# A decoder on one core: stand-in products, half slots and a halved load in the first attention, another order of moves in the later ones

## Chip, cores and metric

One Trainium2 chip, one of its cores. The metric is the time of one launch in microseconds on the device, from the median of several runs. TensorE (PE) multiplies, VectorE (DVE) and ScalarE (ACT) work elementwise, GpSimd (POOL) does little here, and SyncE (SP) issues nearly all DMAs.

## What is computed

A decoder of two layers, for a batch of 4, 512 positions and 256 features, all in float32. Each layer has a self attention, a cross attention to a context of 1024 positions and a third part. The residual stream is normalised ahead of each of the six stages. Cut to what matters here:

```python
# stage A: first attention, 16 heads of 64, rope; per batch element
scores = einsum('hid,hjd->hij', q, k) / 8
kerple = -p * log1p(a * |i - j|)
combined = concat([scores, kerple], over heads)        # 32 numbers per (i, j)
refined = gelu(combined @ w1 + b1) @ w2 + b2           # 32 -> 32 -> 16
out = softmax(causal(scores + kerple + refined)) @ v @ w_o
# stage B: cross attention, 16 heads of 16, 1024 keys, no mask
# stage C: attention with picked experts
# stage D: causal self attention, 16 heads of 16, rope, 512 keys
# stage E: cross attention, 16 heads of 16, 1024 keys, mask, biases
# stage F: 32 routed and 2 shared experts
```

## The kernel before

One hardware loop goes over the four batch elements; a pass runs the stages A to F one after the other, with a barrier of all engines between them. Every engine's instructions are written out by hand, each engine in its own order, and semaphores hold them together. SP's queue is one order too: a wait in it holds all DMAs behind it.

**Stage A** (lines 1332 to 1709). Queries, keys, scores and values come first. The scores of the four query tiles (key lengths L of 512, 384, 256 and 128) are stored to memory and loaded back as chunks, in which a row holds one head and one of 8 queries: 14 chunks, four for each of the three longer tiles and two for the last. Chunks 0 to 7 are of the two long tiles, 8 to 13 of the two short ones. A chunk lies in a slot of `a_fin`, chunk c in slot c % 4 (SP's `load`, line 1438). Its slot is free when the probabilities of the chunk in it before have been turned (line 1456: a wait on `bank_mm`). A chunk of a long tile is worked on in two units, one of a short tile in one: 22 units k. For each unit

- TensorE's `up` (lines 1502 to 1523) multiplies the scores (line 1514) and the distance terms (line 1521) by w1, when the chunk is loaded and the GELU of the unit before is done, because all units use the same four banks;
- ScalarE applies the GELU (line 1628); after the last unit of chunk c it takes the exponentials of chunk c - 1 (line 1618), which have another activation table;
- TensorE's `down` (lines 1525 to 1537) multiplies by w2 into banks 4 and 5, when VectorE has added the unit before (semaphore `mixed`);
- VectorE adds (line 1662), adds the biases and takes maxima (line 1668), and later scales by the inverse sums (line 1681).

Two chunks later TensorE turns the probabilities (line 1545, `turn`), VectorE copies them (line 1698), and when a query tile is complete TensorE weights the values (line 1555) and multiplies by w_o (line 1561). `turn_banks` writes this order out. In TensorE's main loop, step k runs up(k + 1), down(k) and then the turns and values that belong to the step; in the short tiles down(k) comes ahead of up(k + 1).

**Stages B, D, E** (`Attn16`, line 99, and the functions `a16_*`). TensorE projects keys and queries in tiles of 128 x 512; ScalarE copies each tile to `val` (lines 637 and 639), in stage D VectorE applies the rope instead. VectorE splits each tile into three bf16 parts: `parts` (lines 702 to 705) casts, subtracts, casts, subtracts, into KP and QP. SP moves the parts of every group of heads into the stacks KS and QS, six DMAs for a group (`a16_sp`, line 429), in the order of `self.moves` (line 114): t is the half of the heads, gr a group of 2, 2 or 4 heads. In `moves` of before that is, for each t, k0, k1, q0, q1, k2, q2. A wait for the split tile stands ahead of each group. The first score product of a group waits for its keys' and queries' twelve moves (line 506). OT lies over QP and KP, so ScalarE's first copy into it (line 681) waits for all 72 moves.

`keep_warm(count)` (line 399) issues products of 128 x 128 by 128 x 512 in bf16 whose result nobody reads, here called stand-ins. Before the first scores of B, D and E there are `WARM_STACK = 8` of them, behind a wait for all copies of V and all of `val`:

```python
pe.wait_ge(g("v_up"), c.nj // 2)
pe.wait_ge(g("val"), len(c.tiles))
keep_warm(WARM_STACK)
```

Of the kernel before, what the change touches and what calls it, by code (L numbers as in the profile page):

```python
# [98 lines left out]
class Attn16:  # L99


    def __init__(self, name, nk, causal, masked, rope, cross):
# [8 lines left out]
        else:  # L111
            self.tiles = [(kind, t, 0) for t in range(2) for kind in "kq"]
            self.split_order = [0, 1, 2, 3]
        self.moves = [(kind, t, gr) for t in range(2) for kind, gr in (("k", 0), ("k", 1), ("q", 0), ("q", 1), ("k", 2), ("q", 2))]
        self.step = 2 if rope else 1
# [19 lines left out]
    def bank(self, e):  # L135

        return 2 + e % 4 if self.cross else self.step * e % 6

    def pairs_at(self, t):
# [43 lines left out]
NE, NSH = 32, 2  # L183
WARM_LN, WARM_T, WARM_STACK = 22, 6, 8
NRING = 6
# [28 lines left out]
def decoder(nc, io, out, rounds=B):  # L214
    ctx = ExitStack()
    with ctx:
# [80 lines left out]
        for c in CFG:  # L297
            if c in STAGES:
                for n in ("proj", "val", "split", "v_mm", "v_up", "v_zero", "k_ones", *(f"stack_in{gr}" for gr in GROUP_AT.values()), "slot_mm", "slot_free",
                          "m_parts", "m_mm", "m_row", "st_mm", "exp", "pv", "o_up", "recip", "y_mm"):  # L300

                    sm[c, n] = sm["B", n] if c == "D" and "B" in STAGES else sem(f"{n}_{c}")
# [324 lines left out]
        def a16_act(act, c, n):  # L627
            m = M16
            g = lambda s: sm[c.name, s]
            def val(e):  # L630
                kind, t, f = c.tiles[e]
                act.wait_ge(g("proj"), e + 1)
                if e >= NVAL:
                    act.wait_ge(g("split"), e - NVAL + 1)
                o = m["val"][:, e % NVAL, :]
                if c.masked:
                    nc.scalar.activation(o, ps[:, c.bank(e), :], ACT.Identity, bias=(bqE if kind == "q" else bkE)[:, t:t + 1]).then_inc(g("val"), 1)
                else:
                    nc.scalar.activation(o, ps[:, c.bank(e), :], ACT.Copy).then_inc(g("val"), 1)
# [56 lines left out]
        def a16_dve(dve, ch, c):  # L696
            m = M16
            g = lambda s: sm[c.name, s]

            def parts(dst, src, rest, last_sem):  # L700

                ch.link(nc.vector.tensor_copy(dst(0), src))
                ch.link(nc.vector.tensor_tensor(rest, src, dst(0), ALU.subtract))
                ch.link(nc.vector.tensor_copy(dst(1), rest))
                nc.vector.tensor_tensor(dst(2), rest, dst(1), ALU.subtract).then_inc(last_sem, 1)

            for k, e in enumerate(c.split_order):
# [14 lines left out]
                dst = (lambda a: m["QP"][:, a, t, :]) if kind == "q" else (lambda a: m["KP"][:, a, t, f * BANK:(f + 1) * BANK])  # L722
                parts(dst, m["val"][:, e % NVAL, :], m["rest"][:, :], g("split"))

# [542 lines left out]
        def f_dve(dve, ch, n, st):  # L1267
# [58 lines left out]
            for i in range(NI):  # L1326
# [14 lines left out]
        BACK = 504  # L1341
        A_UP, A_DOWN, A_TURN = 0, 4, 6

        sk = [nc.dram_tensor(f"scores{i}", (AU * AH, AQ * (i + 1) * P), F32, kind="Internal").ap() for i in range(NI)]
        named("A", "rope", "qk_mm", "qk_up", "s_mm", "s_up", "v_mm", "v_up", "out0", "out1", "out2", "out3", "fin0", "fin1", "fin2", "fin3",
              "w1", "gelu", "w2", "mixed", "negm", "exp", "prob", "bank_mm", "bank_up")
# [5 lines left out]
        def a1_mem(sb2):  # L1352
# [19 lines left out]
                    M2["fin"][:, 1, 0:4 * TRI_L[3]]]  # L1372
        M1 = M2

        def chunk(n):
# [34 lines left out]
        DOWN_FIRST = [FIRST[c + 1] - 1 for c in range(NCHUNK - 1) if FIRST[c + 1] == LAST[c + 1]]  # L1410

        A_BANKS, BANKS_TO = turn_banks()
        BANK_OF = {u: k for k, u in enumerate(A_BANKS)}
# [8 lines left out]
        def a_sp(sp, b, n, st):  # L1422
# [38 lines left out]
        def a_pe(pe, _, n, st):  # L1461
# [40 lines left out]
            def up(k):  # L1502
                c, q0 = A_UNITS[k]
                i, r, _, L = chunk(c)
                R = SA_R[i]
                if k == FIRST[c]:
                    pe.wait_ge(g(f"fin{c % 4}"), 16 * (c // 4 + 1))
                if k:
                    pe.wait_ge(g("gelu"), k)
                for e in range(4):  # L1510
                    rows = slice(32 * e, 32 * e + 32)
                    for b in range(2):
                        first = (q0 + b * R) * L
                        nc.tensor.matmul(ps[64 * b:64 * b + 64, A_UP + e, 0:R * L], w1A[rows, 0, :], m["fin"][rows, c % 4, first:first + R * L],  # L1514
                                         start=True, stop=False, tile_position=(32 * e, 64 * b), skip_group_check=True)
# [23 lines left out]
            def turn(y, c, k):  # L1539
                _, _, _, L = chunk(c)  # L1540
                q0, j = A_TURNS[c][k]
                if k == 0:
                    pe.wait_ge(g("prob"), c + 1)
                for q in range(4):
                    last = nc.tensor.transpose(ps[:, A_TURN + y % 2, q * P:(q + 1) * P],
                                               m["fin"][:, c % 4, (q0 + q) * L + j * P:(q0 + q) * L + (j + 1) * P], ident[:, :])
                last.then_inc(g("bank_mm"), 1)
# [48 lines left out]
        def a_act(act, _, n, st):  # L1596
# [16 lines left out]
            def weights(c):  # L1613
                _, _, R, L = chunk(c)
                act.wait_ge(g("negm"), c + 1)
                for q in range(R):
                    row = m["fin"][:, c % 4, q * L:(q + 1) * L]
                    nc.scalar.activation(row, row, ACT.Exp, bias=m["nm"][:, c % 4, q:q + 1],  # L1618
# [14 lines left out]
        def a_dve(dve, ch, n, st):  # L1633
# [20 lines left out]
            def refined(k):  # L1654
# [4 lines left out]
                for b in range(2):  # L1659
                    first = q0 + b * R  # L1660
                    rows = m["fin"][:, slot, first * L:(first + R) * L]
                    nc.vector.tensor_tensor(rows, rows, ps[:, A_DOWN + b, 0:R * L], ALU.add).then_inc(g("mixed"), 1)  # L1662
                for b in range(2):
                    dve.wait_ge(g("mixed"), 2 * k + b + 1)
                    for q in range(q0 + b * R, q0 + b * R + R):
                        row = m["fin"][:, slot, q * L:(q + 1) * L]
                        t0 = BACK - i * P - AU * (r + q)
# [6 lines left out]
            def normal(c):  # L1674
# [4 lines left out]
                for q in range(R):  # L1679
                    row = m["fin"][:, slot, q * L:(q + 1) * L]  # L1680
                    last = nc.vector.tensor_scalar(row, row, m["den"][:, slot, q:q + 1], None, ALU.mult)
# [379 lines left out]
```

## Time and profile before

| | us |
|---|---|
| median of 3 runs | 4386.22 (4375.98 to 4389.01) |
| the profiled execution's own time | 4387.44 |
| its span | 4385.7 |
| TensorE matmul busy in it | 3846.2 (88%) |
| TensorE weight loads | 1821.0 (42%) |
| VectorE | 2457.8 (56%) |
| ScalarE | 1682.7 (38%) |
| GpSimd | 152.1 (3%) |
| mean granted TensorE clock, share of full | 0.932 |

The busy time of TensorE counts pipelined products, so it is an upper mark. "Granted clock" is the share of full speed, 2.4 GHz, that TensorE was given; it has two levels, the other is 1.2 GHz. One pass takes about 1,085 us, of which stage A takes some 260, B 177, C 117, D 118, E 204 and F 200. Times in the trace count from the span's start.

### The profile page before, as it was taken

How to read it: one execution, taken by the hardware profiler on the slowest of the kernel's cores; microseconds unless marked ns; L12 is line 12 of the kernel's file. 1: busy time of each engine (PE TensorE's matmuls, PEld its weight loads, DVE VectorE, ACT ScalarE, POOL GpSimd, SP SyncE). 2: the span in 40 equal slices, each digit the busy share in tenths (PEclk: the TensorE clock that was granted, in tenths of full speed). 3: DMA queues.
4: the chain of work that ended last, by engine and by line, in shares of the span. 5: the costliest groups of instructions: out<-in, count | busy, mean ns of one | idle time of the engine just before them, and what ended most of it. 6: DMA issues, size and time to landing. Idle time of an engine off the chain costs nothing.

```text
span 4385.7 us, 57351 instructions
## 1 busy us (share of the span) xinstructions
PE 3846.2 (88%) x21858; PEld 1821.0 (42%) x21938; DVE 2457.8 (56%) x6129; ACT 1682.7 (38%) x2508; POOL 152.1 (3%) x168
## 2 busy tenths in 40 slices
PE   5788888999878888899987898889998789888999
PEld 2352444345435244435533424443553342443355
DVE  5557565742365766573236675657324666666632
ACT  2744433431263443352127254225213726422511
POOL 1000020000000002000000000100000000200000
PEclk9998988999989899899999899889999989988999
DMA  5312002022321200202241210120324121012031
GB/s 180 107 37 55 17 21 51 16 90 72 124 71 41 51 17 26 51 11 98 69 143 53 51 35 17 42 45 1 105 62 152 49 58 24 18 42 45 1 112 59
DMA packets 134703, 254.40 MB, mean 58 GB/s; under 512 B 23269, under 2 KB 82661, under 8 KB 128997
## 3 DMA queue, kind: packets, MB, share of 16 engines
q1 hardware_dynamic: 134408, 250.50, 20.3%
q8 instruction: 182, 2.98, 0.3%
q14 instruction: 113, 0.92, 0.1%
HBM read 156.04 MB, written 44.04 MB: 46 GB/s over the span
## 4 chain that ended last, share of the span: by engine, by line
PE 67%; DVE 15%; ACT 6%; SPq 5%; DMA 3%; issue 3%; POOL 0%; DVEq 0%; POOLq 0%; ACTq 0%
PE ps L1207 11%; PE ps L578 7%; PE ps L1225 5%; PE ps L561 5%; SPq L429 5%; DVE mx L732 5%; PE ps L506 4%; PE ps L1555 3%; DVE ps L729 3%; PE ps L1473 3%; PE ps L402 2%; DMA a_fin<-scores 2%; ACT a_X L1628 2%; PE ps L1514 2%; PE ps L566 2%
## 5 line engine op out<-in xcount | busy, mean ns | idle before, releaser
L670 ACT ACTIVATE PT<-ps 128x1024 f32<-128x1024 f32 (+3 forms) x640 | 605.3, 959 | 480.8 <-PE ps L566 238.2
L506 PE MATMUL ps<-KS,QS 96*128 96x512 bf16 (+3 forms) x1280 | 473.7, 410 | 112.3 <-DVE mx L732 52.4
L732 DVE TENSOR_REDUCE mx<-ps 128x1 f32<-128x512 f32 (+3 forms) x768 | 438.1, 619 | 177.7 <-PE ps L506 87.5
L1207 PE MATMUL ps<-xnT,f_w 128*128 128x512 f32 x1088 | 488.8, 592 | 0.0
L561 PE MATMUL ps<-QS,KS 99*128 99x512 bf16 (+2 forms) x1280 | 431.9, 382 | 10.4 <-ACT QS L660 6.2
L729 DVE CUSTOM_DVE_ANT_0 ps<-ps,mneg 128x512 f32<-128x512 f32 x512 | 342.1, 715 | 136.8 <-PE ps L506 135.1
L578 PE MATMUL ps<-PT,VP 128*32 128x512 f32 (+3 forms) x2560 | 390.9, 593 | 18.4 <-ACT OT L681 18.1
L1313 DVE TENSOR_TENSOR f_tm<-f_si,ps 128x512 f32<-128x512 f32 x128 | 88.0, 687 | 491.6 <-ACT f_si L1265 491.5
L1265 ACT ACTIVATE f_si<-ps 128x512 f32<-128x512 f32 x136 | 80.8, 597 | 594.9 <-PE ps L1220 575.8
L506 PEld LDWEIGHTS ps<-KS,QS 96*128 96x128 bf16 x1280 | 131.6, 103 | 416.3 <-DVE mx L732 196.7
L1207 PEld LDWEIGHTS ps<-xnT,f_w 128*128 128x128 f32 x1088 | 205.9, 190 | 203.4 <-issue 197.1
L561 PEld LDWEIGHTS ps<-QS,KS 99*128 99x128 bf16 x1280 | 110.8, 99 | 389.6 <-issue 191.5
L1225 PE MATMUL ps<-f_w,f_gu 128*128 128x256 f32 x1088 | 264.0, 386 | 9.5 <-DVE f_gu L1314 9.5
L1514 PE MATMUL ps<-a_fin,w1A 32*64 32x512 f32 (+1 forms) x1408 | 107.6, 669 | 160.2 <-ACT a_X L1628 88.4
L1225 PEld LDWEIGHTS ps<-f_w,f_gu 128*128 128x128 f32 x1088 | 210.0, 194 | 83.3 <-issue 43.7
L1628 ACT ACTIVATE a_X<-ps,b1A 128x2048 f32<-128x2048 f32 (+1 forms) x88 | 159.6, 1814 | 210.0 <-PE ps L1521 209.7
L1662 DVE TENSOR_TENSOR a_fin<-a_fin,ps 128x512 f32<-128x512 f32 (+1 forms) x176 | 104.5, 635 | 226.3 <-PE ps L1535 225.5
L660 ACT ACTIVATE QS<-ps 3x512 bf16<-3x512 f32 x192 | 113.3, 590 | 249.9 <-PE ps L544 246.9
L566 PE MATMUL ps<-mnegT,identb 128*128 128x512 bf16 x460 | 179.6, 390 | 0.0
L1473 PE MATMUL ps<-wbuf,a_Y 128*128 128x512 f32 x256 | 129.5, 649 | 24.0 <-issue 22.6
L402 PE MATMUL ps<-mneg,identb 128*128 128x512 bf16 x492 | 127.4, 414 | 24.1 <-DVE val L716 10.6
L1618 ACT ACTIVATE a_fin<-a_fin,a_nm 128x512 f32<-128x512 f32 (+3 forms) x256 | 140.6, 550 | 7.3 <-DVE a_nm L1672 6.7
(272 smaller groups left out, 5419.9 us busy)
## 6 DMA issues: line engine op xcount, KB each, us to landing
f_w<-in_wF SPq DMA_DIRECT2D x136, 384.0 KB, 3.1
scores<-a_fin SPq DMA_DIRECT2D x64, 256.0 KB, 3.0
a_fin<-scores SPq DMA_DIRECT2D x16, 1024.0 KB, 7.9
a_Y<-in_wA SPq DMA_DIRECT2D x5, 3072.0 KB, 14.9
KS<-KP SPq DMA_DIRECT2D x240, 64.0 KB, 2.6
scores<-a_fin SPq DMA_DIRECT2D x64, 192.0 KB, 3.1
a_fin<-scores SPq DMA_DIRECT2D x16, 768.0 KB, 4.3
a_fin<-scores SPq DMA_DIRECT2D x24, 512.0 KB, 3.6
```

The costliest lines, as they stand in the source:

```text
L429: sp.dma_start(stack[HD * r:HD * (r + 1), 8 * t + first:8 * t + first + width, 0:n], parts[HD * first:HD * (first + width), a, t, 0:n]).th ...
L506: last = nc.tensor.matmul(o, m["QS"][0:KR, h, i * P:(i + 1) * P], m["KS"][0:KR, h, f:f + w], start=True, stop=not c.causal)
L561: last = nc.tensor.matmul(o, m["KS"][0:KST, h, j * P:(j + 1) * P], m["QS"][0:KST, h, q0:S], start=True, stop=plain)
L566: last = nc.tensor.matmul(o, identb[:, :], mnegT[:, j, :], start=False, stop=True)
L578: last = nc.tensor.matmul(ps[r:r + 32, 6, q0:S], m["VP"][:, j, h, :], m["PT"][:, mp % 2, j % 2, e, 0:S - q0], start=(j == 0), stop=(j == c ...
L670: nc.scalar.activation(m["PT"][:, mp % 2, j % 2, :, 0:w], ps[:, b0:b0 + 2, 0:w], ACT.Exp, scale=HD ** -0.5).then_inc(g("exp"), 1)
L729: nc.vector.tensor_tensor_reduce(ps[:, k % 2, 0:w], ps[:, k % 2, 0:w], mneg[:, i, f:f + w], 1.0, NEG, ALU.add, ALU.max, m["mx"][:, h % 2, ...
L732: nc.vector.tensor_reduce(m["mx"][:, h % 2, i, f // BANK:f // BANK + 1], ps[:, k % 2, 0:w], AX.X, ALU.max, negate=True).then_inc(g("slot_f ...
L1207: last = nc.tensor.matmul(ps[:, 2 * v + e % 2, :], m["w"][:, e % NRING, (2 * v + k) * P:(2 * v + k + 1) * P], xnT[:, k, :], start=(k == 0) ...
L1225: last = nc.tensor.matmul(ps[:, 6 + i // 2, (i % 2) * DM:(i % 2 + 1) * DM], m["gu"][:, e % 2, i * P:(i + 1) * P], m["w"][:, e % NRING, 2 * ...
L1473: last = nc.tensor.matmul(ps[:, 4 + e % 4, :], m["w"][:, k, col:col + P], xnTA[:, k, :], start=(k == 0), stop=(k == KD - 1))
L1628: nc.scalar.activation(m["hid"][k % 2][:, :, 0:w], ps[:, A_UP:A_UP + 4, 0:w], ACT.Gelu, bias=b1A[:, 0:1]).then_inc(g("gelu"), 1)
```

## The change

It has four parts.

1. Stage A, stand-ins: 14 ahead of the first unit, behind the fifth copy of V (`WARM_LOAD`), and nine (`WARM_EXP`) at the start of step k for k = 4, 6, 8, 10, 12, 14, 16 (`EXP_GAPS`), ahead of up(k + 1), behind a wait for VectorE's additions of unit k - 1. All write bank 4.
2. Stage A, loads: chunk 0 is loaded in two halves with a semaphore each; unit 1 waits for the second. Chunks 8 to 13 lie two in a slot (8 and 9 in slot 0, 10 and 11 in slot 1, 12 and 13 in slot 2), each with a semaphore of its own, and their loads wait for the turns of chunk 4, 4, 5, 5, 6, 6 instead of 4, 5, 6, 7, 8, 9.
3. Stages B, D and E: the moves go k0, q0, k1, q1, k2, q2. Before the first scores there are 3 stand-ins instead of 8.
4. Stages B and E: ScalarE casts the first bf16 part straight from PSUM, ahead of its copy to `val`: for keys in both, for queries in B only. VectorE leaves that cast out and waits for ScalarE's instead.

```diff
-        self.moves = [(kind, t, gr) for t in range(2) for kind, gr in (("k", 0), ("k", 1), ("q", 0), ("q", 1), ("k", 2), ("q", 2))]
+        self.moves = [(kind, t, gr) for t in range(2) for kind, gr in (("k", 0), ("q", 0), ("k", 1), ("q", 1), ("k", 2), ("q", 2))]
...
+    def cast_by_act(self, kind):
+
+        return self.cross and (kind == "k" or not self.masked)
...
-WARM_LN, WARM_T, WARM_STACK = 22, 6, 8
+WARM_LN, WARM_T, WARM_STACK = 22, 6, 3
...
                 o = m["val"][:, e % NVAL, :]
+                if c.cast_by_act(kind):
+                    top = m["QP"][:, 0, t, :] if kind == "q" else m["KP"][:, 0, t, f * BANK:(f + 1) * BANK]
+                    if c.masked:
+                        nc.scalar.activation(top, ps[:, c.bank(e), :], ACT.Identity, bias=bkE[:, t:t + 1]).then_inc(g("cast"), 1)
+                    else:
+                        nc.scalar.activation(top, ps[:, c.bank(e), :], ACT.Copy).then_inc(g("cast"), 1)
...
-                ch.link(nc.vector.tensor_copy(dst(0), src))
+                if not cast:
+                    ch.link(nc.vector.tensor_copy(dst(0), src))
...
-                parts(dst, m["val"][:, e % NVAL, :], m["rest"][:, :], g("split"))
+                if c.cast_by_act(kind):
+                    dve.wait_ge(g("cast"), e + 1)
+                parts(dst, m["val"][:, e % NVAL, :], m["rest"][:, :], g("split"), c.cast_by_act(kind))
...
+        WARM_EXP, WARM_LOAD = 9, 14
...
+        SMALL = min(n for n, (i, _) in enumerate(CHUNKS) if i < 2)
+
+        def loaded(c):
+
+            return f"fin{c % 4 if c < SMALL else c}"
+
+        def fin(c):
+
+            if c < SMALL:
+                return M2["fin"][:, c % 4, :]
+            half = (c - SMALL) % 2 * (CH_MAX // 2)
+            return M2["fin"][:, (c - SMALL) // 2, half:half + CH_MAX // 2]
...
+        EXP_GAPS = [LAST[c] + 1 for c in range(1, SMALL)]
...
-                sp.dma_start(M2["fin"][:, c % 4, 0:R * L], sk[i][:, r * L:(r + R) * L]).then_inc(g(f"fin{c % 4}"), 16)
+                if c == 0:
+                    sp.dma_start(fin(c)[:, 0:R * L // 2], sk[i][:, r * L:r * L + R * L // 2]).then_inc(g(loaded(c)), 16)
+                    sp.dma_start(fin(c)[:, R * L // 2:R * L], sk[i][:, r * L + R * L // 2:(r + R) * L]).then_inc(g("fin_half"), 16)
+                else:
+                    sp.dma_start(fin(c)[:, 0:R * L], sk[i][:, r * L:(r + R) * L]).then_inc(g(loaded(c)), 16)
...
             for c in range(4, NCHUNK):
-                sp.wait_ge(g("bank_mm"), BANK_OF["turn", c - 4, len(A_TURNS[c - 4]) - 1] + 1)
+                left = c - 4 if c < SMALL else 4 + (c - SMALL) // 2
+                sp.wait_ge(g("bank_mm"), BANK_OF["turn", left, len(A_TURNS[left]) - 1] + 1)
                 load(c)
...
-                if k == FIRST[c]:
-                    pe.wait_ge(g(f"fin{c % 4}"), 16 * (c // 4 + 1))
+                if k == 1:
+                    pe.wait_ge(g("fin_half"), 16)
+                elif k == FIRST[c]:
+                    pe.wait_ge(g(loaded(c)), 16 if c >= SMALL else 16 * (c // 4 + 1))
...
+            pe.wait_ge(g("v_up"), 5)
+            keep_warm(WARM_LOAD, bank=A_DOWN)
             pe.wait_ge(g("s_up"), 4 * NI)
             up(0)
             pe.wait_ge(g("v_up"), 8)
             for k in range(NU + 4):
+                if k in EXP_GAPS:
+                    pe.wait_ge(g("mixed"), 2 * k)
+                    keep_warm(WARM_EXP, bank=A_DOWN)
```

What is left out replaces `m["fin"][:, c % 4, ...]` by `fin(c)[:, ...]` in `up`, `turn`, the exponentials and VectorE's functions, and names the new semaphores.

## Rows read from the trace of the kernel before

**Rows 1.** Windows of the first attention, a line per pass; columns: first line
```profile
core 0: us, PE busy (x) PEld busy (x) DVE busy (x) ACT busy (x) POOL busy (x), PEclk, DMA share, GB/s
53.00:312.00 259.00, 211.18 (x2117) 105.97 (x2115) 142.17 (x382) 136.76 (x203) 0.00 (x0) 0.96 0.29 91
1131.00:1401.00 270.00, 222.00 (x2112) 108.53 (x2112) 142.26 (x382) 135.55 (x201) 0.00 (x0) 0.89 0.28 89
2216.00:2483.00 267.00, 216.93 (x2112) 106.82 (x2112) 142.01 (x382) 135.56 (x201) 0.00 (x0) 0.91 0.28 91
3301.00:3565.00 264.00, 214.33 (x2112) 106.28 (x2112) 142.26 (x382) 135.57 (x201) 0.00 (x0) 0.92 0.29 92
```

**Rows 2.** Waits: who for whom; us in total, times, longest
```profile
PE ps L1514 <- DMA a_fin<-scores: 71.8, 24, 4.0
```

**Rows 3.** Timeline of ScalarE, second pass: start us, us, engine, line, operation
```profile
1225.31 1.28 ACT L1618 ACT_TABLE_LOAD   x1
...
1230.85 1.97 ACT L1628 ACTIVATE a_X<-ps,b1A 128x2048 f32<-128x2048 f32 x1
```

**Rows 4.** Timeline of TensorE, second pass; in brackets idle before and releaser
```profile
1232.87 2.01 PE L1514 MATMUL ps<-a_fin,w1A 32*64 32x512 f32 x16 [4.44 <-ACT a_X L1628]
...
1293.28 0.90 PE L1514 MATMUL ps<-a_fin,w1A 32*64 32x384 f32 x16
...
1303.79 1.09 PE L1535 MATMUL ps<-a_X,w2A 64*32 64x512 f32 x16
...
1308.56 2.01 PE L1514 MATMUL ps<-a_fin,w1A 32*64 32x512 f32 x16 [3.68 <-DMA a_fin<-scores]
```

**Rows 5.** The timeline of TensorE: the first unit of passes one and three
```profile
126.94 1.12 PE L1514 MATMUL ps<-a_fin,w1A 32*64 32x512 f32 x16 [2.88 <-DMA a_fin<-scores]
...
2292.77 1.50 PE L1514 MATMUL ps<-a_fin,w1A 32*64 32x512 f32 x16 [4.00 <-DMA a_fin<-scores]
```

**Rows 6.** The timeline of the first cross attention, second pass
```profile
1410.96 7.58 SPq L429 DMA_DIRECT2D KS<-KP  x12
...
1414.84 0.69 DVE L705 TENSOR_TENSOR QP<-rest,QP 128x512 bf16<-128x512 f32 x1
...
1418.59 7.57 SPq L429 DMA_DIRECT2D QS<-QP  x12
...
1419.46 0.60 ACT L643 ACTIVATE VP<-ps 128x512 f32<-128x512 f32 x1 [1.13 <-PE ps L469]
...
1423.74 0.60 PE L506 MATMUL ps<-KS,QS 96*128 96x512 bf16 x2 [1.74 <-DMA QS<-QP]
```

**Rows 7.** The timeline of the second cross attention: its stand-ins
```profile
1838.38 1.67 PE L402 MATMUL ps<-mneg,identb 128*128 128x512 bf16 x7 [0.92 <-ACT VP L643]
```

**Rows 8.** The timeline of the self attention, second pass
```profile
1710.62 7.64 SPq L429 DMA_DIRECT2D KS<-KP  x12
...
1714.53 0.69 DVE L705 TENSOR_TENSOR QP<-rest,QP 128x512 bf16<-128x512 f32 x1
...
1759.55 0.59 ACT L681 ACTIVATE OT<-ps 64x512 f32<-64x512 f32 x1 [6.41 <-DMA QS<-QP]
```

**Rows 9.** The chain of waits in order of time: 21 stand-ins
```profile
489.22 4.70 PE ps L402 x21
```

**Rows 10.** The timeline of VectorE in an exponentials' gap
```profile
1242.63 1.28 DVE L1662 TENSOR_TENSOR a_fin<-a_fin,ps 128x512 f32<-128x512 f32 x2 [0.34 <-PE ps L1535]
```

**Rows 11.** Windows, lines 1514, 1521: units 0-16, last two sums 17-21
```profile
126.00:216.00 90.00, 18.19 (x272) 4.31 (x272) 0.96 0.26 85
...
sum 376.00, PE 78.74 PEld 17.68; mean PE 19.69 PEld 4.42
126.00:216.00 90.00, 17.53 (x288) 7.16 (x288) 0.96 0.26 85
...
sum 376.00, PE 79.18 PEld 29.76; mean PE 19.80 PEld 7.44
...
sum 245.00, PE 28.88 PEld 5.32; mean PE 7.22 PEld 1.33
sum 245.00, PE 31.42 PEld 23.45; mean PE 7.85 PEld 5.86
```

More of the change, by code:

```diff
@@ L298, in decoder @@
             if c in STAGES:
-                for n in ("proj", "val", "split", "v_mm", "v_up", "v_zero", "k_ones", *(f"stack_in{gr}" for gr in GROUP_AT.values()), "slot_mm", "slot_free",
+                for n in ("proj", "cast", "val", "split", "v_mm", "v_up", "v_zero", "k_ones", *(f"stack_in{gr}" for gr in GROUP_AT.values()), "slot_mm", "slot_free",
                           "m_parts", "m_mm", "m_row", "st_mm", "exp", "pv", "o_up", "recip", "y_mm"):
@@ L698, in a16_dve, with parts @@
             g = lambda s: sm[c.name, s]
-            def parts(dst, src, rest, last_sem):
-                ch.link(nc.vector.tensor_copy(dst(0), src))
+            def parts(dst, src, rest, last_sem, cast=False):
+                if not cast:
+                    ch.link(nc.vector.tensor_copy(dst(0), src))
                 ch.link(nc.vector.tensor_tensor(rest, src, dst(0), ALU.subtract))
@@ L1342, in decoder @@
         A_UP, A_DOWN, A_TURN = 0, 4, 6
+        WARM_EXP, WARM_LOAD = 9, 14
         sk = [nc.dram_tensor(f"scores{i}", (AU * AH, AQ * (i + 1) * P), F32, kind="Internal").ap() for i in range(NI)]
-        named("A", "rope", "qk_mm", "qk_up", "s_mm", "s_up", "v_mm", "v_up", "out0", "out1", "out2", "out3", "fin0", "fin1", "fin2", "fin3",
+        named("A", "rope", "qk_mm", "qk_up", "s_mm", "s_up", "v_mm", "v_up", "out0", "out1", "out2", "out3", "fin0", "fin1", "fin2", "fin3", "fin_half", *(f"fin{c}" for c in range(8, 14)),
               "w1", "gelu", "w2", "mixed", "negm", "exp", "prob", "bank_mm", "bank_up")
@@ L1513, in up @@
                         first = (q0 + b * R) * L
-                        nc.tensor.matmul(ps[64 * b:64 * b + 64, A_UP + e, 0:R * L], w1A[rows, 0, :], m["fin"][rows, c % 4, first:first + R * L],
+                        nc.tensor.matmul(ps[64 * b:64 * b + 64, A_UP + e, 0:R * L], w1A[rows, 0, :], fin(c)[rows, first:first + R * L],
                                          start=True, stop=False, tile_position=(32 * e, 64 * b), skip_group_check=True)
@@ L1545, in turn @@
                     last = nc.tensor.transpose(ps[:, A_TURN + y % 2, q * P:(q + 1) * P],
-                                               m["fin"][:, c % 4, (q0 + q) * L + j * P:(q0 + q) * L + (j + 1) * P], ident[:, :])
+                                               fin(c)[:, (q0 + q) * L + j * P:(q0 + q) * L + (j + 1) * P], ident[:, :])
                 last.then_inc(g("bank_mm"), 1)
@@ L1616, in weights @@
                 for q in range(R):
-                    row = m["fin"][:, c % 4, q * L:(q + 1) * L]
+                    row = fin(c)[:, q * L:(q + 1) * L]
                     nc.scalar.activation(row, row, ACT.Exp, bias=m["nm"][:, c % 4, q:q + 1],
@@ L1660, in refined @@
                     first = q0 + b * R
-                    rows = m["fin"][:, slot, first * L:(first + R) * L]
+                    rows = fin(c)[:, first * L:(first + R) * L]
                     nc.vector.tensor_tensor(rows, rows, ps[:, A_DOWN + b, 0:R * L], ALU.add).then_inc(g("mixed"), 1)
@@ L1665, in refined @@
                     for q in range(q0 + b * R, q0 + b * R + R):
-                        row = m["fin"][:, slot, q * L:(q + 1) * L]
+                        row = fin(c)[:, q * L:(q + 1) * L]
                         t0 = BACK - i * P - AU * (r + q)
@@ L1679, in normal @@
                 for q in range(R):
-                    row = m["fin"][:, slot, q * L:(q + 1) * L]
+                    row = fin(c)[:, q * L:(q + 1) * L]
                     last = nc.vector.tensor_scalar(row, row, m["den"][:, slot, q:q + 1], None, ALU.mult)
```

## The prediction

> **What bounds the kernel now.** I read the windows of the first attention first. Its four passes differ by ten microseconds although they do the same work: the granted clock of TensorE is 0.96 of full speed in the first and 0.89, 0.91 and 0.92 in the others [rows 1]. Then the waits: the first product of a unit (line 1514) waits 71.8 us for its chunk's scores from memory, 24 times, up to 4.0 us [rows 2]. Then the order of time. ScalarE goes from the GELU to the exponentials of the chunk before and back, with a table load of 1.28 us on each side [rows 3], and TensorE has nothing to do meanwhile: it sat idle 4.44 us before 1232.87 us [rows 4], and the next products took 2.01 us for sixteen instead of the 1.12 us of [rows 5], which is 1.2 GHz instead of 2.4. The next GELU needs these products, so the slow clock lies on the path. In the small tiles (key lengths 256 and 128) the idle time belongs to the loads: 3.68 us before 1308.56 us [rows 4]. In the cross attentions the first score product waits for moved queries [rows 6], in the second one for the eight stand-ins [rows 7]. In the self attention the OT copy waits 6.41 us for the last moved queries [rows 8]: there the queue of moves is the bound.
>
> All sums are made against the profiled execution, 4387.44 us (span 4385.7), 1 us above the median of the three runs shown. A measurement of this kernel tells about 0.3%, 13 us, from no change.
>
> **The change, part by part.** In the first attention a stand-in product costs 4.70/21 = 0.224 us at full clock [rows 9].
>
> *Exponentials' gaps.* Nine stand-ins are 2.0 us. They are placed ahead of the next unit's products at seven places, behind a wait for VectorE's two additions of the unit before. Those take 1.28 us and start 0.34 us after their releaser at 1242.63 us [rows 10]. At the first five places 1.3 + 2.0 = 3.3 us stands against an idle time of 4.44 us [rows 4]; in the later gaps TensorE's turns of an earlier chunk fill the wait for VectorE, so that 2.0 us stands against an idle time that is shorter by about as much. So I cost these five at nothing; what covers them is ScalarE's table loads and exponentials, and without that cover each costs 2.0 us. What they give back is the clock. The unit products of lines 1514 and 1521 took 78.74 + 79.18 = 157.9 us over four passes up to the small tiles. The first pass took 18.19 + 17.53 = 35.7 us [rows 11] with one unit at half clock, worth 2 x (2.01 - 1.12) = 1.8 us, so 33.9 us at full clock. Recovered: 157.9 - 4 x 33.9 = **-22.3 us**. Bounds: 0 and 22.3.
>
> At the last two places there is no gap: the unit product at 1293.28 us follows without idle time, and at the other the path goes through the products at 1303.79 us [rows 4]. There 2 x 2.0 x 4 = **+16 us** goes on TensorE's own path (bounds 0, if a load still waits behind it, and 16).
>
> *First load in two.* It waited 2.88 to 4.00 us [rows 5]. Fourteen stand-ins, 3.1 us, now stand in the same place, so the half that lands sooner can't start anything sooner: mean wait 3.4 against 3.1, **-1 us** (bounds: 0 to -4). The next late thing is the stand-ins themselves. One more issue on SP, about 0.6 us, moves the stores behind it; nobody waits for those before the third chunk. The Trainium skill, "DMA: Bandwidth & Descriptors", section Bandwidth, says to batch transfers to 1 MiB or more for three quarters of the peak, which speaks against halving a 1 MiB load; by it the halving costs rather than gains; priced with one more issue of 0.63 us per pass (an estimate from [rows 6]) the sum would be 2.5 us larger.
>
> *Small tiles in half slots.* The six last chunks lie two in a slot, and their loads wait for the turns of chunks 4, 4, 5, 5, 6, 6 instead of 4 to 9: from the second on they are issued one to three chunks earlier. Of the 71.8 us, four first loads are 4 x 3.4 = 13.6; the other 20 waits, **-58.2 us**, go [rows 2, 5]. What is late next: ScalarE's chain per chunk (GELU 1.97, two table loads, exponentials) is shorter than TensorE's chain of turns, values and units, so TensorE itself bounds; I count no new wait. With the idle time goes half clock: these 20 units took 28.88 + 31.42 = 60.3 us [rows 11] against 20 x 2.22 = 44.4 at full clock, **-15.9 us**. Bounds for both together: -74 and, if VectorE or ScalarE is found directly behind, half of it, -37.
>
> First attention: -22.3 + 16 - 1 - 58.2 - 15.9 = -81.4 us.
>
> *First cross attention, four times.* SP issues twelve moves in 7.6 us, 0.63 each. Now the six query moves come after six key moves instead of twelve, and the queries are split by 1415.5 us [rows 6]. ScalarE's cast goes ahead of its copy (0.60 us, the form of its copy at 1419.46), VectorE drops a copy that can't cost more than its subtraction's 0.69, say 0.5; with the key casts ahead, the copies of the normed input slip by some 0.4 us. So queries are split at 1416.0 and issued by 1419.8. Before, the sixth issue ended at 1418.59 + 3.8 = 1422.4 and the product came 1.36 us later; now at 1421.2. TensorE's own way is equally long: V's last copy ends at 1420.06, plus 0.4, plus three stand-ins (0.7), 1421.2. Against 1423.74: -2.5, take -2.4. The later groups' issues end 0.9 us later than before, but the third head's scores stand behind sixteen tiles of VectorE's maxima, and need them later than that. **-9.6 us** (bounds 0 and -4 x 3.8).
>
> *Second cross attention.* Its first scores came right behind the stand-ins, which came behind V's last copy [rows 7]; five fewer are 1.1 us. The queries keep their VectorE cast. **-4.4 us** (bounds 0 and -4.4).
>
> *Self attention.* It gets the new order too, and no ScalarE cast. Six key moves end at 1710.62 + 3.8 = 1714.4; queries are split at 1715.2 [rows 8]. SP stands 0.8 to 0.9 us in that wait, everything queued behind it is later by so much, and the OT copy waits for the last of it. Fewer stand-ins gain nothing, as VectorE's splitting ends no sooner. **+3.6 us** (bounds 0 and 4).
>
> Sum: -81.4 - 9.6 - 4.4 + 3.6 = -91.8; 4387.4 - 91.8 = 4295.6, **4296 us**.
>
> **Rivals.**
> 1. *The clock is not kept.* Stand-ins have an idle time of about 1 us on both sides, and the granted clock could still fall. Against it: the first pass, with the same gaps and no stand-ins, still has 0.96. Without term one: 4296 + 22 = 4318. Chance 0.12.
> 2. *A next limiter in the small tiles.* The loads come early but VectorE (additions, maxima, inverse, turn copies) takes their place; nothing in the waits shows it yet, because the loads come last. Half of 58 lost: 4296 + 29 = 4325; if the queue still hands the loads over late (the change then doesn't do what it says), all 58, 4354. Chance 0.15 and 0.02.
> 3. *Queries gain nothing,* the new order costing at the second group what it gives at the first: +14, 4310. Chance 0.06.
> 4. *All half-clock time is paid.* In the passes of [rows 1] time at 1.2 GHz is 2 x (1 - clock) x length: 21 + 59 + 48 + 42 = 170 us, some 30 of them at the stage's start and not touched. If the other 140 cost half their length on the path, 70 comes back where I count 38: 4264. Against it: 38 us more of it lengthened the second pass by 11 only (270 against 259), some of that at its start. "TensorE: Matmul & The Clock Gate", section Terms, in the Trainium skill gives that rule, the penalty being half the throttled time. Chance 0.05.
> 5. *Slower: stand-ins run at half clock and overrun.* Each batch is then 3.9 us, the first 6. Five gaps overrun by 1.6 us each (8), two places cost 3.9 each (8), the start 2.6: 18.4 per pass, 74. No clock comes back, half of the load waits (-29) and the first cross attention (-10) do: 4387 + 74 - 39 = 4422. It decides where a batch costs more than about 2.7 us. Against it: the unit before each gap ran at full clock in the rows. Chance 0.02.
>
> **How the numbers follow.** The forecast, 4296 with its own range 4278 to 4314, has 0.58. The range goes down to 4274 (loss at the two full places hidden, more slow clock returned) and up to 4338 (rivals 1 to 3 and a part of two together). Faster 0.96, same 0.02, slower 0.02.
>
> **What would show it.** Right: the clock of the first attention at 0.95 or more in all passes; no or nearly no wait of line 1514 for a load; units of 2.0 to 2.2 us after every gap; passes of some 236 to 246 us, within a few us of each other; first scores of the first cross attention 20 us after its k_unit issue, not 22.6; the OT copy of the self attention waiting longer. Wrong: line 1514 waiting for VectorE or ScalarE in the small tiles; line 402 at 0.43 us each in the gaps; the later unit products behind them late by more than 2 us.

## The result, and the profile after

The kernel after the change takes 4281.57 us, the median of four runs (4278.10 to 4283.78); beside it the kernel before took 4386.44 us (4375.98 to 4389.01). The ratio is 0.9765, with a 95% interval of 0.9747 to 0.9782: 105 us faster, where 92 were forecast. The time lies in the range and 14 us below the forecast. The profiled execution took 4281.05 us, so the difference of the two profiled executions is 106.4 us.

The head of the page of the kernel after (span, busy time of each engine, and the chain that ended last by engine and line):

```profile
span 4279.3 us, 57827 instructions
...
PE 3843.3 (90%) x22074; PEld 1828.7 (43%) x22186; DVE 2438.5 (57%) x6089; ACT 1702.1 (40%) x2548; POOL 152.0 (4%) x168
...
PE 71%; DVE 15%; ACT 7%; SPq 4%; issue 3%; DMA 0%; DVEq 0%; POOLq 0%; ACTq 0%
```

TensorE is busy as long as before (3846.2 us then), the added stand-ins included, and the share of the chain that passes through transfers is 0% where it was 3%; SP's own issues still have 4%. I cut the profile into stages at issues on SP's queue: the weights of B, which are issued as A begins; the unit constants of B, D and E (`in_k_unit`); the weights of D, issued as C begins; the copy of x for F, which ends with the store of x. Each entry is the sum over the four passes:

| us | A | B | C | D | E | F |
|---|---|---|---|---|---|---|
| before | 1046.8 | 709.7 | 466.7 | 473.3 | 827.0 | 788.3 |
| after | 965.9 | 695.7 | 461.4 | 475.6 | 817.7 | 788.4 |
| difference | -80.9 | -14.0 | -5.3 | +2.3 | -9.3 | +0.1 |
| forecast | -81.4 | -9.6 | 0 | +3.6 | -4.4 | 0 |

The first attention came out as summed. The windows of the first attention of the kernel after, a line per pass, answer to [rows 1]:

```profile
54.00:297.00 243.00, 222.66 (x2185) 110.76 (x2191) 141.49 (x382) 136.69 (x203) 0.00 (x0) 0.99 0.30 97
1112.00:1353.00 241.00, 219.44 (x2181) 109.52 (x2189) 141.78 (x382) 135.56 (x201) 0.00 (x0) 0.99 0.31 98
2166.00:2410.00 244.00, 221.83 (x2181) 110.67 (x2189) 141.62 (x382) 135.55 (x201) 0.00 (x0) 0.97 0.30 97
3225.00:3466.00 241.00, 220.75 (x2176) 109.74 (x2185) 141.36 (x381) 135.56 (x201) 0.00 (x0) 0.97 0.31 98
```

The granted clock, the first number behind POOL's, is 0.97 to 0.99 in all four; before it was 0.96, 0.89, 0.91 and 0.92. The lengths of A by pass, 240.2 to 242.8 us, differ by 3 us instead of 10 (256.7 to 266.7). The timeline of TensorE in the second pass shows a gap with stand-ins, then the two full places, then the small tiles; lines 1550, 1557, 1571, 1581 and 406 are what 1514, 1521, 1535, 1545 and 402 were:

```profile
1206.11 1.89 PE L406 MATMUL ps<-mneg,identb 128*128 128x512 bf16 x8 [1.68 <-DVE a_fin L1703]
1208.87 1.12 PE L1550 MATMUL ps<-a_fin,w1A 32*64 32x512 f32 x16 [0.87 <-ACT a_X L1669]
...
1261.39 0.66 PE L1581 MATMUL ps<-ident,a_fin 128*128 128x128 f32 x4
1262.10 1.89 PE L406 MATMUL ps<-mneg,identb 128*128 128x512 bf16 x8
1263.92 0.90 PE L1550 MATMUL ps<-a_fin,w1A 32*64 32x384 f32 x16
...
1273.88 0.66 PE L1581 MATMUL ps<-ident,a_fin 128*128 128x128 f32 x4
1274.59 1.89 PE L406 MATMUL ps<-mneg,identb 128*128 128x512 bf16 x8
1276.41 1.09 PE L1571 MATMUL ps<-a_X,w2A 64*32 64x512 f32 x16
1277.43 1.11 PE L1550 MATMUL ps<-a_fin,w1A 32*64 32x512 f32 x16
...
1286.10 1.11 PE L1550 MATMUL ps<-a_fin,w1A 32*64 32x512 f32 x16
...
1295.13 1.11 PE L1550 MATMUL ps<-a_fin,w1A 32*64 32x512 f32 x16
...
1305.51 1.11 PE L1550 MATMUL ps<-a_fin,w1A 32*64 32x512 f32 x16
...
1312.50 1.11 PE L1550 MATMUL ps<-a_fin,w1A 32*64 32x512 f32 x16
```

In the gap at 1206.11 the stand-ins wait 1.68 us for VectorE, and behind them 0.87 us are still idle: they cost nothing, and the unit takes 1.12 us instead of the 2.01 of [rows 4]. At 1262.10 and 1274.59 they have no bracket: TensorE was busy until then and is busy at once after, so each puts some 1.8 us on its own path. In the small tiles no unit waits for a load or runs at 1.2 GHz; the 3.68 us before a unit in [rows 4] are gone.

The first cross attention, second pass: the queue of SP, ScalarE's first cast and copy, and the first scores, answering to [rows 6]:

```profile
1353.29 0.29 SPq L425 DMA_DIRECT2D KS<-in_k_unit  x1
1355.25 0.60 ACT L645 ACTIVATE KP<-ps 128x512 bf16<-128x512 f32 x1 [29.25 <-PE ps L462]
1355.74 0.59 ACT L649 ACTIVATE val<-ps 128x512 f32<-128x512 f32 x1
...
1362.13 3.79 SPq L433 DMA_DIRECT2D KS<-KP  x6
...
1367.68 3.74 SPq L433 DMA_DIRECT2D QS<-QP  x6
...
1372.87 0.60 PE L510 MATMUL ps<-KS,QS 96*128 96x512 bf16 x2
```

Six query moves now follow six key moves, and the first product starts 1372.87 - 1353.29 = 19.58 us after the k_unit issue, where it took 22.56. The cast's record says 0.60 us, but the copy behind it starts 0.49 us later: records of one engine overlap, and the step is what a cast costs.

### The profile page after: what moved, and what is told of

Read it like the earlier page. It is cut to its first block, busy times and chain, and to the rows that moved or that the text cites. A ratio compares the mean times of both kernels' runs of the same rounds, so it can differ in the third digit from the quotient of the medians.

```text
span 4279.3 us, 57827 instructions
## 1 busy us (share of the span) xinstructions
PE 3843.3 (90%) x22074; PEld 1828.7 (43%) x22186; DVE 2438.5 (57%) x6089; ACT 1702.1 (40%) x2548; POOL 152.0 (4%) x168
## 4 chain that ended last, share of the span: by engine, by line
PE 71%; DVE 15%; ACT 7%; SPq 4%; issue 3%; DMA 0%; DVEq 0%; POOLq 0%; ACTq 0%
PE ps L1220 11%; PE ps L582 7%; PE ps L1238 6%; PE ps L565 5%; DVE mx L745 5%; PE ps L510 4%; SPq L433 4%; PE ps L1591 3%; PE ps L406 3%; DVE ps L742 3%; PE ps L1507 3%; ACT a_X L1669 2%; PE ps L462 2%; PE ps L570 2%; PE ps L1531 2%
## 5 line engine op out<-in xcount | busy, mean ns | idle before, releaser
L406 PE MATMUL ps<-mneg,identb 128*128 128x512 bf16 x708 | 169.2, 387 | 39.4 <-DVE a_fin L1703 15.0
L1507 PE MATMUL ps<-wbuf,a_Y 128*128 128x512 f32 x256 | 129.1, 648 | 24.1 <-issue 22.7
L765 DVE RECIPROCAL rq<-ps 128x16 f32<-128x16 f32 x48 | 12.3, 257 | 228.2 <-PE ps L520 228.2
```

The lines of the kernel that those rows point to most:

```text
L406: nc.tensor.matmul(ps[:, bank, :], identb[:, :], mneg[:, 0, 0:BANK], start=True, stop=True)
L1507: last = nc.tensor.matmul(ps[:, 4 + e % 4, :], m["w"][:, k, col:col + P], xnTA[:, k, :], start=(k == 0), stop=(k == KD - 1))
```

## Experiments

Each edit is made on the kernel after, and nothing that any of these kernels computes changes: they differ in stand-ins, in the size and time of transfers and in which engine casts. Ratios are to the kernel before on the same chip. Because the later stages vary by themselves (first run below), I read each edit from the length of its own stage, summed over four passes, and use the time as a check.

**The same kernel again.**

> The changed kernel once more, unchanged. The forecast missed 14 us outside the first attention: stages B and E gained 14.0 and 9.3 us in the profile where 9.6 and 4.4 were forecast, and stage C, whose code is the same, gained 5.3. Theory one (the phase of the clock's steps against the work is chance): total 4282 within 6 us, and the lengths of C, D and E differ between the two profiles of the same code by 1 to 3 us in single passes. Theory two (the change itself keeps the clock better there): all stage lengths repeat within 0.5 us in each pass.

4284.28 us (4282.62 to 4286.02), ratio 0.9769 (0.9744 to 0.9794). A is 966.0 against 965.9, E 817.7 both times. But B is 699.4 against 695.7, C 464.0 against 461.4, D 472.6 against 475.6. Two windows of the same self attention, second pass, of the kernel after and of its repeat:

```profile
1641.00:1762.00 121.00, 102.90 (x639) 53.90 (x641) 67.96 (x185) 38.50 (x60) 2.13 (x3) 0.87 0.13 38
```

```profile
1647.00:1764.00 117.00, 101.39 (x639) 52.95 (x638) 67.60 (x184) 38.54 (x60) 2.13 (x3) 0.88 0.13 40
```

The same 639 products take 120.4 us at a granted clock of 0.87 in one and 117.3 at 0.88 in the other. So a difference of 3 us in one of these stages between two traces proves nothing. In seven profiles that share the later code, B ranges from 695.7 to 699.4 (mean 696.7), C from 461.4 to 467.7 (465.1), D from 472.6 to 480.5 (475.8), E from 812.8 to 818.6 (816.4).

Two more spreads bear on what follows. A has the same code in six profiles (this one, its repeat and the four kernels below that change only B, D or E): 965.9 to 968.4, mean 967.0. And three further kernels (the old order in the self attention alone, and the two that join the parts) also have B's unchanged code: B came out at 694.5, 693.3 and 691.3 there. So over ten profiles identical code of B takes 691.3 to 699.4, mean 695.6.

**Full slots in the small tiles, stand-ins kept.**

```diff
-        SMALL = min(n for n, (i, _) in enumerate(CHUNKS) if i < 2)
+        SMALL = NCHUNK
-        EXP_GAPS = [LAST[c] + 1 for c in range(1, SMALL)]
+        EXP_GAPS = [LAST[c] + 1 for c in range(1, 8)]
```

> The small tiles' chunks in full slots again (loads wait for the turns of chunks 4 to 9), all stand-ins kept. My terms: the waits 58.2 and half clock 15.9 come back, less 8 because the stand-ins of the last place then stand in a load's wait: 4282 + 66 = 4348. Rival (next limiter, half of the waits were never to be had): 4282 + 37 = 4319.

4349.31 us, ratio 0.9919 (0.9894 to 0.9944). Stage A is 1031.1: the half slots are worth 65.2 us (64.1 against the mean of six). The waits of this kernel (who for whom; us in total, times, longest):

```profile
PE ps L1550 <- DMA a_fin<-scores: 48.1, 20, 3.4
```

Without the half slots twenty waits for loads are back; the kernel after has none in this list. They are 48.1 us and not the 58.2 of the forecast. The stand-ins at the full places fill part of the time in which the loads are late: unit 17, right behind the last of them, waits 0.6 to 0.7 us here in each pass, where it waited 3.3 to 3.9 in the kernel before.

**No stand-ins in the gaps.**

```diff
-        EXP_GAPS = [LAST[c] + 1 for c in range(1, SMALL)]
+        EXP_GAPS = [LAST[c] + 1 for c in range(1, 1)]
```

> No stand-ins at all seven places of the exponentials' gaps, the 14 at the first load stay. My terms: 22.3 of clock lost, 16 on TensorE's path saved: 4282 + 6 = 4288. Rival one (all half-clock time is paid, half of its length): units after gaps and everything behind them, 4282 + 30 - 16 = 4296. Rival two (the gaps keep the clock without them, as in the first pass of before): 4282 - 16 = 4266.

4285.40 us (4276.94 to 4289.06), ratio 0.9765 (0.9738 to 0.9791): the seven batches together are worth next to nothing, 3.0 us in stage A (968.9), and only 1.9 against the mean of six. TensorE's timeline in this kernel, second pass, three exponentials' gaps:

```profile
1210.91 2.01 PE L1550 MATMUL ps<-a_fin,w1A 32*64 32x512 f32 x16 [4.44 <-ACT a_X L1669]
...
1235.49 1.23 PE L1550 MATMUL ps<-a_fin,w1A 32*64 32x384 f32 x16 [3.42 <-ACT a_X L1669]
...
1246.75 1.59 PE L1550 MATMUL ps<-a_fin,w1A 32*64 32x384 f32 x16 [2.96 <-ACT a_X L1669]
```

The idle time and the slow unit of [rows 4] are back at 1210.91. The units of 384 take 0.91 us at full clock (the next run shows one) and 1.59 at 1.2 GHz, so at 1246.75 the whole unit is slow and at 1235.49 part of it. Of the 20 units behind the five real gaps of the four passes, 9 are slow throughout, 2 in part and 9 run at full clock.

**Stand-ins in the first five gaps alone.**

```diff
-        EXP_GAPS = [LAST[c] + 1 for c in range(1, SMALL)]
+        EXP_GAPS = [LAST[c] + 1 for c in range(1, 6)]
```

> Stand-ins only at the first five places (k = 4 to 12), not at k = 14 and 16 where TensorE had no idle time. My term: 2 x 2.0 us x 4 passes less on TensorE's path: 4282 - 16 = 4266. Rival (they are hidden there, or the clock needs them): 4282 within 4 us.

4270.80 us (4269.94 to 4275.03), ratio 0.9741 (0.9716 to 0.9766); stage A 951.4. The two full places cost 965.9 - 951.4 = 14.5 us, four times 2 x 1.8, and the five real gaps give 968.9 - 951.4 = 17.5. Against the mean of six the full places cost 15.6. This is how two halves of one idea cancelled in the run above. At the place of the first full batch nothing now stands between the turns and the unit (timeline of TensorE, this kernel):

```profile
1258.50 0.66 PE L1581 MATMUL ps<-ident,a_fin 128*128 128x128 f32 x4
1259.09 0.90 PE L1550 MATMUL ps<-a_fin,w1A 32*64 32x384 f32 x16
```

**The old order of moves in the self attention alone.**

```diff
-        self.moves = [... (("k", 0), ("q", 0), ("k", 1), ("q", 1), ("k", 2), ("q", 2))]
+        self.moves = [... that order if cross, else (("k", 0), ("k", 1), ("q", 0), ("q", 1), ("k", 2), ("q", 2))]
```

> The self attention (stage D) moves k0, k1, q0, q1, k2, q2 again; the cross attentions keep the new order. My term: SP no longer stands 0.9 us in the wait for q0, so the last move lands 0.9 us sooner and ScalarE's first OT copy with it: 4282 - 3.6 = 4278, stage D 0.9 us shorter in each pass. Rival (D is longer because three stand-ins instead of eight let the clock fall ahead of its scores): OT copy sooner, but stage D still 120.4 us in some passes.

4278.21 us (4275.29 to 4280.48), ratio 0.9767 (0.9732 to 0.9801). The number was met, but this pair does not show the reason: D is 473.3, inside the span of the unchanged code (472.6 to 480.5). The first OT copy starts 64.5 us after the stage's k_unit issue here, 64.6 in the kernel after, 63.9 in the kernel before (means of four passes). The order moves it by 0.1 us in this pair; the next part looks at all kernels.

**No casts on ScalarE.**

```diff
-        return self.cross and (kind == "k" or not self.masked)
+        return False
```

> ScalarE casts nothing, VectorE casts all first parts again; all else as changed. By my accounting of the first cross attention the cast costs ScalarE 0.6 us ahead of its copy and saves VectorE 0.46 per tile: queries split at the same time, so within 2 us of 4282; only the keys' moves start 0.9 us later. Rival (VectorE's splitting of six tiles is what the first maximum waits for): first maximum of stage B 2.3 us later, 4282 + 9 = 4291.

4283.64 us (4282.55 to 4285.95), ratio 0.9781 (0.9747 to 0.9815): the casts are worth nothing that shows in the time. The first product of B starts after 19.58 us in every pass, as with them. What the casts do shows in the key moves of B, which start 8.85 us after the k_unit issue with them and 9.78 without; with the new order no product waits for that. B is 699.8, just above the ten profiles with casts (691.3 to 699.4), so that some microseconds may be theirs; this run can't tell.

**Eight stand-ins before the first scores.**

```diff
-WARM_LN, WARM_T, WARM_STACK = 22, 6, 3
+WARM_LN, WARM_T, WARM_STACK = 22, 6, 8
```

> Eight stand-ins ahead of the first scores instead of three, in B, D and E. My terms: five times 0.22 = 1.1 us on TensorE's path in B and E, none in D: 4282 + 8.8 = 4291. Rival (they keep the clock in D): stage D 117 to 118 us in all passes, no 120.4, 3 us less of it: 4288.

4288.99 us (4288.27 to 4295.40), ratio 0.9791 (0.9757 to 0.9825). The first product comes after 20.66 us in B (+1.08) and after 27.17 in E (+1.08, one pass 28.41). B is 701.6, E 823.1. The five stand-ins lie on the path in both cross attentions, as soon as the queries don't come last. The timeline of E in this kernel, second pass:

```profile
1765.24 0.27 SPq L425 DMA_DIRECT2D KS<-in_k_unit  x1
...
1790.67 1.90 PE L406 MATMUL ps<-mneg,identb 128*128 128x512 bf16 x8 [0.69 <-ACT VP L653]
1792.40 0.60 PE L510 MATMUL ps<-KS,QS 96*128 96x512 bf16 x2
```

**The old order of moves everywhere.**

```diff
-        self.moves = [... (("k", 0), ("q", 0), ("k", 1), ("q", 1), ("k", 2), ("q", 2))]
+        self.moves = [... (("k", 0), ("k", 1), ("q", 0), ("q", 1), ("k", 2), ("q", 2))]
```

> The old order of moves in all three attentions, casts by ScalarE and three stand-ins kept. My terms: B's first scores wait for the queries behind twelve key moves again, +2.4 to 3.0 us each (less 0.9 for the earlier start of the keys' moves), E none, D -0.9: 4282 + 4 x (2.1 - 0.9) = 4287. Rival (the order is worth nothing, the casts bring B's gain): 4278.

4287.21 us (4285.17 to 4289.69), ratio 0.9788 (0.9754 to 0.9822). B's first product waits for the queries again, and comes 21.69 us after the k_unit issue (the start of B in this kernel, second pass):

```profile
1355.17 0.29 SPq L425 DMA_DIRECT2D KS<-in_k_unit  x1
1364.02 7.60 SPq L433 DMA_DIRECT2D KS<-KP  x12
1371.67 7.57 SPq L433 DMA_DIRECT2D QS<-QP  x12
...
1376.86 0.61 PE L510 MATMUL ps<-KS,QS 96*128 96x512 bf16 x2 [1.94 <-DMA QS<-QP]
```

So in B the new order alone gives 21.69 - 19.58 = 2.11 us a pass at the start (B is 701.8, 6.2 above the mean of ten). With the old order the product waits for the queries' moves, not for the stand-ins; it still comes 0.9 us sooner than in the kernel before (22.58), as the key moves do. E starts at 26.09 with either order, for it waits for V. D is 470.4 here, the lowest of all by 0.1.

**No stand-ins at the start of A**, with the first load in halves, and with the first load whole:

```diff
-        WARM_EXP, WARM_LOAD = 9, 14
+        WARM_EXP, WARM_LOAD = 9, 0
```

The second of the two kernels has this as well, and unit 1 no longer waits for a second half:

```diff
-                if c == 0:
+                if c < 0:
```

> No stand-ins ahead of the first unit; the first load still in two halves. My theory: the fourteen stand-ins (2.97 us in the trace) end about when the half lands, so taking them away leaves an idle time of nearly the same length; the first unit starts 0 to 1 us sooner and its products may run at half clock (+1 us each time). Time 4282 (4278 to 4286). Rival: the stand-ins outlast the half load and are themselves the bound at the start; then the first unit starts over 1 us sooner in each pass and the time is 4277 or less. The first product's idle time tells them apart: 2.5 to 3 us by the theory, under 2 us by the rival.

> No stand-ins ahead of the first unit and the first load whole again, as before the change. Together with the run with the halves it gives the worth of the halving alone. My theory: the whole chunk lands 0.3 to 1 us later than the half, so that this kernel is 1 to 4 us slower than the one with the halves: 4285 (4282 to 4289), idle time ahead of the first product 3.4 us as in the kernel before. Rival: the halving costs one more issue on the queue of SP and gains nothing; then this one is as fast or up to 2.5 us faster, 4280.

4283.75 us (4279.15 to 4286.75), ratio 0.9771 (0.9750 to 0.9792) with the halves; 4287.29 us (4285.98 to 4291.52), ratio 0.9783 (0.9763 to 0.9804) with the load whole. The waits of both, halves first:

```profile
PE ps L1550 <- DMA a_fin<-scores: 8.8, 4, 3.0
```

```profile
PE ps L1548 <- DMA a_fin<-scores: 12.8, 4, 4.0
```

The mean idle time is 2.2 us with halves, between my two conditions, and 3.2 whole. Stage A is 961.4 with halves, 967.6 whole, and 965.9 in the kernel after. So the halving alone is worth 6.2 us in these two profiles, of which the shorter wait is 4 x 1.0; the rest is no more than A's own spread of 2.5. The fourteen stand-ins that came with it take 4.5 back: in the kernel after, the half has landed 0.7 to 1.7 us before the first unit starts, and they are still running. The time of the first run hides this gain: its C and D came out at 467.5 and 480.5, the upper end of what unchanged code shows.

**The parts together:** five gaps and the old order in D, with and without the stand-ins at the start of A.

> The best of the parts together: stand-ins in the first five gaps alone, the old order of moves in the self attention, the new one in the cross attentions. By my sum the two full places gave 11 us (the run with five gaps) to 16 us (forecast) and the old order in the self attention up to 4: 4268 (4264 to 4271). Rival: the order in the self attention is worth nothing, because its stage length is set by where the half-clock spells fall: 4271, the time of the run with five gaps.

> The run with five gaps and the old order in the self attention, and no stand-ins ahead of the first unit. Effects add, so it stands to that run as the run without stand-ins at the start stands to the kernel after: 4268 (4264 to 4272), within 4 us of it. Rival: the stand-ins at the start hold the clock for the gaps behind them, and without them units of the first chunks fall to half clock: 4 us or more slower than with them.

With them 4267.02 us, the median of five runs between 4261.15 and 4272.37 (a sixth took 12453 us, for a reason that is not on record; with it the median is 4268.97), ratio 0.9737 (0.9716 to 0.9758). Without them **4258.22 us** (4257.77 to 4261.39), ratio 0.9717 (0.9697 to 0.9737): 23 us faster than the kernel after, 21 by the ratios to the kernel before on the same chip. Stage A is 951.8 and 946.5: -5.3 for the start, as -4.5 above, so these effects add. My expectation of times within 4 us of each other was wrong, and so was its rival, which had it slower. The medians differ by 8.8 us; the 3.5 that stage A doesn't hold stay unexplained, within what the other stages vary by themselves. The windows of A in the faster one show that the clock holds without stand-ins at the start:

```profile
56.00:292.00 236.00, 214.17 (x2153) 107.58 (x2159) 142.03 (x383) 135.51 (x201) 0.00 (x0) 0.99 0.31 100
1104.00:1340.00 236.00, 213.74 (x2153) 107.61 (x2159) 142.06 (x383) 135.74 (x201) 0.00 (x0) 0.98 0.31 100
2155.00:2394.00 239.00, 215.55 (x2153) 108.78 (x2159) 142.35 (x383) 135.73 (x201) 0.00 (x0) 0.97 0.31 99
3210.00:3446.00 236.00, 214.20 (x2153) 107.37 (x2158) 142.17 (x383) 135.46 (x201) 0.00 (x0) 0.98 0.31 100
```

## Why the prediction was right, and where it missed

**The five gaps: right, the term too large.** Forecast -22.3, measured -17.5. The cover held (0.87 us idle behind the stand-ins). The forecast took the products of the two lines up to the small tiles from 157.9 us to the 135.6 of full clock, and credited all of it to the gaps. The same products (now lines 1550 and 1557, windows that hold units 0 to 16 of each pass) take 77.0 + 77.9 us without stand-ins in gaps and 69.7 + 68.8 with the five:

```profile
sum 374.88, PE 76.95 PEld 17.30; mean PE 19.24 PEld 4.32
sum 374.88, PE 77.88 PEld 29.19; mean PE 19.47 PEld 7.30
...
sum 357.29, PE 69.65 PEld 16.86; mean PE 17.41 PEld 4.21
sum 357.29, PE 68.76 PEld 28.13; mean PE 17.19 PEld 7.03
```

So the gaps' stand-ins gave back 154.8 - 138.4 = 16.4, nearly the whole of the 17.5 on the path. Of the other 5.9, 3.1 were gone without them and 2.8 stay: they lie in units near the stage's start, such as the second of the first pass with 1.57 us, where no gap's stand-ins reach. Rival 1, the clock not kept, fell with the clock of 0.97 to 0.99.

**The two full places: right.** Forecast +16, measured +14.5. Against the mean of six profiles it is +15.6. The step that there is no gap, read from a unit without a bracket in [rows 4], is what carried it.

**First load: right in mechanism, the size within the noise.** Forecast -1; the kernel after against the one with neither halves nor stand-ins is 965.9 - 967.6 = -1.7, which A's spread of 2.5 us covers. The stand-ins are the next late thing, as the forecast said. The Trainium skill ("DMA: Bandwidth & Descriptors", section Bandwidth) advises large transfers, and the forecast priced the halving by it at +2.5 us. This case doesn't show that: on its own the halving gains 6, since the first unit needs only half of the megabyte and waits 2.2 us instead of 3.2.

**The small tiles: right.** Forecast -58.2 - 15.9 = -74.1. The stage's -80.9, less -17.5, +14.5 and -1.7, leaves -76.2. Undoing the half slots measured 65.2. The difference fits full places that are cheap while loads are late: the kernel with full slots is 1046.8 - 1031.1 = 15.7 us below before in A, of which the gaps and the start are 19.2, so that 3.5 remain for the two full places there instead of 14.5. This 3.5 is a remainder of the same lengths and no measurement of its own; what is seen is the wait behind the last batch, 0.6 to 0.7 us instead of 3.3 to 3.9. It is near the bound of 0 that the forecast gave them, "if a load still waits behind it". Rival 2, VectorE or ScalarE directly behind, did not appear: no unit waits for either in the small tiles.

**First cross attention: right mechanism, the term too small.** Forecast -2.4 a pass, measured -3.00 at the first product (22.58 to 19.58). The step that was off is the cast: I let it delay V's copies by 0.4 us and the split queries by 0.5. The first query move is issued 14.40 us after the k_unit issue with casts and 14.37 without, and the product behind V's last copy starts at 19.58 in both. The parts don't add one by one: the casts' earlier key moves gave 0.9 with the old order and nothing with the new one, the new order 2.11 with three stand-ins, and five fewer stand-ins 1.08 once it is there. The stage gained 10.3 to 18.4 over the ten profiles with this code, 14.1 in the mean. Rival 3, the order gaining nothing, fell with this: with the old order B is 6.2 us longer than the mean of the ten.

**Second cross attention: the term that was mis-sized.** Forecast -1.1 a pass from [rows 7], which is the second pass, measured -2.24 (28.41 to 26.17 at the first product). In the other three passes of before the eight stand-ins took about twice as long, at 1.2 GHz, as this row of the timeline of the kernel before shows for the first pass:

```profile
750.98 3.15 PE L402 MATMUL ps<-mneg,identb 128*128 128x512 bf16 x7 [1.09 <-ACT VP L643]
```

They took 3.15 us instead of 1.67. I had read one pass of four and taken it for all; that is -4.5 of the -4.9 by which the stage beat its term.

**Self attention: the term neither shown nor refuted.** Forecast +0.9 a pass for SP's wait for the split queries. The OT copy does start 0.65 us later than before (64.56 against 63.91), but with the old order it starts late too: 64.30 to 64.57 in the four kernels that have it, mean 64.43, against 64.36 to 65.25 in the nine with the new order, mean 64.73. So the order accounts for some 0.3 us of the later start, and the rest has another cause, which stays open. The stage itself leans to the forecast: D is 470.4 to 473.6 (mean 472.0) in the four and 472.6 to 480.5 (mean 475.6) in the nine, a difference of 3.6 where 3.6 was forecast, but the two ranges overlap, and the longest passes (120.3 us and more) come with either order, 2 of 16 and 14 of 36.

**Attention with picked experts.** No code changed, and -5.3 us were measured where none was forecast; in the repeat it was -2.7, in the mean of seven profiles -1.6. No gain of the change is shown in it: identical code of this stage took 459.8 to 467.7 us over all thirteen later profiles. The seven-profile means of B, C, D and E together are -22.7 us against before, where -10.4 was forecast: B -3.4, C -1.6, D -1.1, E -6.2 beyond their terms. Before has one trace, so the same unsteadiness is in these too.

**Rival 4, all half-clock time is paid.** Its time, 4264, lies 18 us below the result, mine 14 above, so the total alone hardly tells them apart; stage A came out at my sum. The two kernels with and without stand-ins in the five gaps decide. From the windows of A the time at 1.2 GHz, 2 x (1 - clock) x length over four passes, is about 112 us without and 40 with them (the clocks have two decimals). These 72 us less brought 17.5 back, a quarter. "TensorE: Matmul & The Clock Gate", section Terms, of the Trainium skill would have half, an estimate of 36 us; this case's measurement differs. The products of lines 1550, 1557, 1571 and 1581 together took 394.6 us in A without the stand-ins and 366.5 with them: these 28 us are not far from half, but the stage got only 17.5 shorter. So the clock was paid in the products, and more than a third of that beside the path.

**Rival 5, stand-ins at half clock,** fell too: a batch of nine takes 1.89 us, not 3.9.

## What to carry to other kernels

Put stand-in products only where the trace shows idle time on TensorE on both sides of them, and take them out where the next product has no wait: taking them out at two of seven places and at one start gave 19 of the 23 us by which the best version beats this change. Read every pass before a duration is multiplied by the number of passes. And judge an edit by the length of its own stage, not by the total, when stages that nobody touched vary by several microseconds; and take more than one profile of the same code before a difference of that size is believed, for the stage's own length varies as well.

## What the hardware did that was not expected

Identical code of a stage can take one of a few lengths, not a continuum: the attention with picked experts took 114.5, 116.2 or 117.0 to 117.3 us in every pass of every profile. The self attention is less regular, 116.9 to 119.0 or 120.3 to 121.6; its passes of 120.3 and more had a granted clock of 0.86 to 0.87, those under 118.3 one of 0.88 to 0.90. And ScalarE's 128x512 cast and the copy behind it follow at a step of 0.49 us, though each has a record of 0.60: a sum of recorded durations overstates what an added instruction costs on a busy engine.
